# Message parts stored as consecutive bf16 elements, with the middle part rounded on ScalarE, in a graph network layer

## The reference, cut to what matters

```
msg  = concat([x[dst], edge_attr])            # 206250 x 128
h    = relu(msg @ W1a.T + b1a) @ W1b.T + b1b  # 206250 x 64
sums = segment_sum(h, src, 6250)              # and counts, for the mean
agg  = sums / max(counts, 1)
z    = relu(concat([x, agg]) @ W2a.T + b2a) @ W2b.T + b2b
out  = layernorm(x + concat([z, x]) @ Wr.T + br)
```

## Time and profile before

| | |
|---|---|
| median of 3 runs | 1581.24 us |
| the profiled execution | 1581.64 us, span 1580.0 us |
| PE matmul busy | 1534.2 us, 97% |
| PEld weight load busy | 1261.8 us, 80% |
| DVE busy | 1395.8 us, 88% |
| ACT busy | 942.6 us, 60% |
| POOL busy | 1061.9 us, 67% |
| mean granted TensorE clock | 0.992 |

### The profile page before, as it was taken

How to read it: one execution, slowest core, us unless ns; L and a number is a source line. 1 busy time by engine, 2 the same in 40 slices (tenths; PEclk the granted TensorE clock), 3 DMA queues, 4 the chain that set the end, 5 groups by cost and what they waited for, 6 DMA issues and landing times.

```text
span 1580.0 us, 41462 instructions
## 1 busy us (share of the span) xinstructions
PE 1534.2 (97%) x13337; PEld 1261.8 (80%) x13337; DVE 1395.8 (88%) x3954; ACT 942.6 (60%) x1808; POOL 1061.9 (67%) x929
## 2 busy tenths in 40 slices
PE   9899999999999999999999999999999999995897
PEld 6678878888887887877878788888888888884786
DVE  5799999999989999999988989999999999884886
ACT  2476767677677676767767775555555555563222
POOL 2366667666666676666767778777777777876542
PEclk9999999999999999999999999999999999997999
DMA  7566656666666666666656669889989989866997
GB/s 207 163 163 161 173 158 165 167 165 165 158 174 160 163 173 161 163 167 167 163 157 171 170 166 315 273 279 294 286 281 292 277 271 290 279 193 198 364 364 236
DMA packets 135497, 335.37 MB, mean 212 GB/s; under 512 B 36506, under 2 KB 69565, under 8 KB 129016
## 3 DMA queue, kind: packets, MB, share of 16 engines
q0 software_dynamic: 53184, 224.62, 45.3%
q1 hardware_dynamic: 81028, 104.02, 25.7%
q10 hardware_dynamic: 1076, 4.09, 1.0%
HBM read 213.07 MB, written 119.52 MB: 210 GB/s over the span
## 4 chain that ended last, share of the span: by engine, by line
PE 86%; DMA 4%; POOL 3%; DVE 2%; issue 2%; ACT 1%; SPq 0%; POOLq 0%; DVEq 0%; ACTq 0%
PE HH L543 22%; PE MS L552 18%; PE PA L568 14%; PE PBk L568 13%; PE RK L581 8%; DMA gbuf<-region,idx 3%; POOL region L1295 2%; PE RK L661 2%; PE RK L666 2%; PE CK L628 2%; PE PA L581 2%; DVE OH L1133 1%; DMA kb<-keyd 0%; POOL gbuf L1323 0%; PE PA L700 0%
## 5 line engine op out<-in xcount | busy, mean ns | idle before, releaser
L1295 POOL DMA_INDIRECT region<-stg,dest x806 | 930.5, 1154 | 417.2 <-ACT stg L852 246.8
L552 PE MATMUL MS<-W,hT 128*128 128x64 f32 x3224 | 508.1, 258 | 4.5 <-DVE pos L1017 3.0
L552 PEld LDWEIGHTS MS<-W,hT 128*128 128x128 f32 x3224 | 466.6, 191 | 6.5 <-DVE pos L1017 3.3
L543 PE MATMUL HH<-eab,pw 128*128 128x512 f32 x806 | 433.2, 619 | 1.7 <-ACT hT L806 1.7
L1012 DVE TENSOR_SCALAR M<-pos_of,pos 128x384 bf16<-128x384 int16 x1612 | 409.1, 316 | 0.2
L852 ACT ACTIVATE stg<-PA 120x585 bf16<-120x585 f32 x403 | 266.6, 661 | 184.7 <-PE PA L568 184.3
L568 PE MATMUL PA<-Z,M 128*128 128x195 bf16 x2418 | 354.3, 254 | 3.8 <-DVE M L1012 1.5
L568 PE MATMUL PBk<-Z,M 128*128 128x195 bf16 x2418 | 354.0, 254 | 0.2 <-ACT stg L852 0.2
L568 PEld LDWEIGHTS PA<-Z,M 128*128 128x128 bf16 x2418 | 230.1, 106 | 122.1 <-issue 117.2
L806 ACT ACTIVATE hT<-HH 128x512 f32<-128x512 f32 x403 | 240.8, 598 | 127.4 <-PE HH L543 127.0
L852 ACT ACTIVATE stg<-PBk 120x585 bf16<-120x585 f32 x403 | 266.1, 660 | 51.1 <-PE PBk L568 49.2
(11 more groups left out here) (207 smaller groups left out, 1386.1 us busy)
## 6 DMA issues: line engine op xcount, KB each, us to landing
eab<-in_ea SPq DMA_DIRECT2D x201, 256.0 KB
kb<-keyd SPq DMA_DIRECT2D x201, 128.0 KB
pw<-ptab SPq DMA_DIRECT2D x403, 32.0 KB
region<-stg,dest POOLq DMA_INDIRECT x806
gbuf<-in_xt ACTq DMA_DIRECT2D x6, 422.5 KB
ptab<-OH SPq DMA_DIRECT2D x7, 256.0 KB, 2.4
gbuf<-region,idx POOLq DMA_INDIRECT x98, 8.4
eab<-in_xt SPq DMA_DIRECT2D x12, 130.0 KB
```

The lines of the kernel that those rows point to most:

```text
L543: e.matmul(HH[:, :], pw[:, q % 4, :], eab[:, c % NB, at_q:at_q + GE], start=True, stop=True).then_inc(s_h, 1)
L552: ins = e.matmul(MS[:, o:o + D], hT[:, q % 2, 128 * j:128 * j + 128], W[:, W_1B:W_1B + D], start=True, stop=True)
L1295: e.indirect_dma_start(region[s], bass.IndirectOffsetOnAxis(ap=dest[:, g:g + 1], axis=0), stw[:, g % NS, :], None).then_inc(s_sc[g % NS], 16)
```

## The change

Z becomes a bf16 tile in which the three parts of a message column (65 elements each) are consecutive, [128, 2, 8, 3, 65], so the 195 moving columns of `permute` are contiguous. A float32 tile Zr of one pair holds the remainder.

- `copy_x` and `copy_id` write bf16, so ScalarE rounds the high part.
- `rest` writes MS minus the high part into Zr. It waits in addition for the middle part of the pair before (s_mid), since Zr has one buffer.
- `middle_part` is new on ScalarE: it copies Zr to part 1 as bf16. It stands in the turn after relu(2m), ahead of evict(2m-3).
- `low` waits for s_mid instead of s_r, and writes Zr minus the middle part as bf16. It stands behind the four places of quad 2m-2 and ahead of onehot(m+1).
- The memset of the ones follows the new layout, and there is one more semaphore.

```diff
-        Z = sb("Z", [128, 2, 3, 8, PART])
-        Zb = Z[:, :, :, :, :].bitcast(bf16)
+        Z = sb("Z", [128, 2, 8, 3, PART], bf16)
+        Zr = sb("Zr", [128, 8, D])
...
-                                                Zb[:, q // 2 % 2, :, 4 * (q % 2) + 2 * h + t, 1::2],
+                                                Z[:, q // 2 % 2, 4 * (q % 2) + 2 * h + t, :, :],
...
                     def copy_x(m):
                         n = 4 * of_pair(m)
                         e.wait_ge(s_msg, m + 1)
-                        e.activation(Z[:, m % 2, 0, 0:n, 0:D],
+                        e.activation(Z[:, m % 2, 0:n, 0, 0:D],
                                      MS[:, 0:n * D].rearrange("p (j f) -> p j f", f=D), ACT.Copy).then_inc(s_x, 1)
+
+                    def middle_part(m):
+                        n = 4 * of_pair(m)
+                        e.wait_ge(s_r, m + 1)
+                        e.activation(Z[:, m % 2, 0:n, 1, 0:D], Zr[:, 0:n, :], ACT.Copy).then_inc(s_mid, 1)
...
                             relu(2 * f)
+                        if m - 1 in front:
+                            middle_part(front[m - 1])
...
                         e.wait_ge(s_x, m + 1)
-                        e.tensor_tensor(Z[:, m % 2, 1, 0:n, 0:D],
-                                        MS[:, 0:n * D].rearrange("p (j f) -> p j f", f=D),
-                                        Zb[:, m % 2, 0, 0:n, 1:2 * D:2], ALU.subtract).then_inc(s_r, 1)
+                        if m >= 1:
+                            e.wait_ge(s_mid, m)
+                        e.tensor_tensor(Zr[:, 0:n, :], MS[:, 0:n * D].rearrange("p (j f) -> p j f", f=D),
+                                        Z[:, m % 2, 0:n, 0, 0:D], ALU.subtract).then_inc(s_r, 1)
 
                     def low(m):
                         n = 4 * of_pair(m)
-                        e.wait_ge(s_r, m + 1)
-                        e.tensor_tensor(Zb[:, m % 2, 2, 0:n, 1:2 * D:2], Z[:, m % 2, 1, 0:n, 0:D],
-                                        Zb[:, m % 2, 1, 0:n, 1:2 * D:2], ALU.subtract).then_inc(s_l, 1)
+                        e.wait_ge(s_mid, m + 1)
+                        e.tensor_tensor(Z[:, m % 2, 0:n, 2, 0:D], Zr[:, 0:n, :],
+                                        Z[:, m % 2, 0:n, 1, 0:D], ALU.subtract).then_inc(s_l, 1)
...
                         if m - 1 in front:
                             rest(front[m - 1])
-                            low(front[m - 1])
                         if 0 <= 2 * m - 2 < NQ:
                             places(2 * m - 2, 0)
                             places(2 * m - 2, 1)
+                        if m - 1 in front:
+                            low(front[m - 1])
                         if m + 1 in front:
                             onehot(front[m + 1])
```

More of the change, by code:

```diff
@@ L310, in _ @@
                 e.memset(ind[:, 62:63], 1.0)
-                e.memset(Z[:, :, 1, :, 64:65], 1.0).then_inc(p_t, 1)
+                e.memset(Z[:, :, :, 1, 64:65], 1.0).then_inc(p_t, 1)
             @block.vector
@@ L393, in program @@
          s_oh, s_h, s_relu, s_msg, s_x, s_r, s_l, s_M, s_pA, s_pB, s_eA, s_eB,
-         s_OHv, s_acc, s_ad, s_nt, s_tx, s_zt, s_z1, s_r1, s_y, s_sq, s_var, s_rt, s_fin, s_sw, s_zr, s_zs, s_id, s_P, s_pz, s_pt, s_xr, s_rest) = [
-            sem(f"s{i}") for i in range(47)]
+         s_OHv, s_acc, s_ad, s_nt, s_tx, s_zt, s_z1, s_r1, s_y, s_sq, s_var, s_rt, s_fin, s_sw, s_zr, s_zs, s_id, s_P, s_pz, s_pt, s_xr, s_rest, s_mid) = [
+            sem(f"s{i}") for i in range(48)]
         again = [*s_ch, *s_pw, *s_sc, *s_ga, *s_gb, *s_tab, *s_kw, *s_nx, *s_ob, *s_xo,
@@ L399, in program @@
                  s_oh, s_h, s_relu, s_msg, s_x, s_r, s_l, s_M, s_pA, s_pB, s_eA, s_eB,
-                 s_OHv, s_acc, s_ad, s_nt, s_tx, s_zt, s_z1, s_r1, s_y, s_sq, s_var, s_rt, s_fin, s_sw, s_zr, s_zs, s_id, s_P, s_pz, s_pt, s_xr, s_rest]
+                 s_OHv, s_acc, s_ad, s_nt, s_tx, s_zt, s_z1, s_r1, s_y, s_sq, s_var, s_rt, s_fin, s_sw, s_zr, s_zs, s_id, s_P, s_pz, s_pt, s_xr, s_rest, s_mid]
         TURNS = range(FIRST, NP + 2)
@@ L813, in copy_id @@
                         k = 8 * m % (16 * BQ)
-                        e.activation(Z[:, m % 2, 0, 0:n, D], lid[:, k:k + n], ACT.Copy)
+                        e.activation(Z[:, m % 2, 0:n, 0, D], lid[:, k:k + n], ACT.Copy)
                     def copy_x(m):
```

## The result

The changed kernel takes 1577.47 us (median of 8 runs, 1576.36 to 1579.41), the kernel before, run beside it, 1582.31 us (median of 8). The ratio is 0.9972, 95% interval [0.9961, 0.9983]: faster by 4.4 us, or 0.3%. I had said 12.7 us, and 1569 us. The profiled execution took 1577.92 us, its span is 1576.3 us and its granted clock 0.990 (before 0.992).

What follows compares the result with a forecast made beforehand. TensorE was taken as the bound. Gains of 8.7 us in plain and 6.7 in class-sum turns, less 2.7 in chain turns, make 12.7 us off 1581.64, so 1569 us; the 8-in-10 range was 1554 to 1590.

Steps and rivals of the forecast that it cites:

- P = R+2.38: In a plain turn, permute's start (P) was forecast 2.38 us after the start of rest (R); before the change 2.37.
- The middle part takes 0.63 us and is hidden: ScalarE's new copy of 512 elements from SBUF, 0.60 to 0.66 us, was to end while VectorE does the places.
- Low takes 0.72 and starts at R+1.57: VectorE's low, 750 ns before, was to take 0.72 us, starting 1.57 us after rest starts, behind four places.
- first rival: Low fully hidden: permute's releasers finish before TensorE wants them; gain about 26 us, 1556 us; chance 0.22.
- 5.7 ns for each of 4836 matmuls, 27.6 us: Contiguous columns were to cut each permute matmul on TensorE from 92 to 86.3 ns, 24 matmuls a turn.
- The upper end, 9 ns each: Upper bound of the layout's gain on TensorE, 43 us, if all 195 columns went at 0.43 ns each.
- A plain turn of 6.05, a gain of 0.06 in 145 turns: 8.7 us: Turns without class sum or late chain were to go from 6.11 to 6.05 us, TensorE waiting 0.08 for low.
- 8 chain turns lose 0.33 each, 2.7 us: Turns where a block's chain makes rest late and already held TensorE: permute starts later, each losing 0.33 us.
- a slack of 0.39 us: How much later than needed permute's releasers could come in a plain turn before the change without TensorE waiting.
- 49 class-sum turns gain the whole 0.137, 6.7 us: Turns with 2.6 us of class-sum matmuls ahead of permute: low not late, so TensorE's full layout gain remains.
- the layout buys nothing: Rival: contiguous columns gain TensorE nothing, plain turns 0.01 us longer; 5 us slower, 1586 us; chance 0.15.
- low becomes the bound: Rival: slower middle part and low make permute late, turn 0.10 us longer; 12 us slower, 1593 us; chance 0.20.

Runs made afterwards that it cites:

- e4: Changed kernel with the middle part copied for only 8 of 64 columns, the others left out: 1579.56 us, ratio 0.9986.
- e2: Changed kernel with the new layout alone: order of before, no middle part, low subtracts the high part: 1565.03 us, ratio 0.9887 to the kernel before.
- e1: Changed kernel with low between the two pairs of places instead of behind all four: 1575.19 us, ratio 0.9947 to the kernel before.
- e16: Changed kernel with middle part and low split per quad up to turn 144, first half of low behind two places: 1571.22 us, ratio 0.9931.
- e10: Changed kernel with 8 instead of 120 rows in 99 of 806 scatters: ratio 1.0829 where the kernel before takes 1753 to 1780 us.
- e12: The changed kernel itself, no edit, on a chip where the kernel before takes 1753.34 us: 1887.02 us, ratio 1.0724.

## Why the prediction was right or wrong, point by point

The mechanism held: a layout that speeds TensorE up, and an order that makes it wait for low. Three terms of the sum were mis-sized. The forecast's 153 turns without class sums were to gain 6.0 us, which is 4.7 for turns 20 to 140, and 0.2 were measured there; for 46 class-sum turns to 6.3, and 3.2 were measured. The plain turn gains half of what was put down, because part of the pitch is lost among the messages. The late turns are twice as many as before, where the sum had them as 8. And the class-sum turns don't get the whole pitch.

- **TensorE is the bound and P = R+2.38.** Right: the median of P - R is 2.371 over turns 8 to 141.
- **The middle part takes 0.63 us and is hidden.** Right: 631 ns, and e4 gains nothing by cutting it to 263.
- **Low takes 0.72 and starts at R+1.57.** Errors that cancel, so that P = R+2.38 is luck: it takes 682 ns, starts at R+1.63 in the median (bounds 1.51 to 1.60), and the matmul follows its end by 0.06 and not by 0.09. The start was counted from places of 0.99 us, which is right in the 15 plain turns without a stretched place (R+1.52); in 89 the GpSimd instruction stretches one. Before, most of that stretching seems to have fallen on onehot, which nobody waits for: 115 of its 202 instructions last over 780 ns, each with the end of a GpSimd instruction 489 to 493 ns ahead of its own, and 7 after the change (mean 855 ns, now 756). The prediction moved instructions along VectorE's queue without asking what GpSimd does at their new time. The 15 turns with unstretched places are its first rival come true, low hidden and the turn 6.00 us.
- **5.7 ns for each of 4836 matmuls, 27.6 us.** The pitch is right where permute's matmuls stand together (92 against 86 ns), but half of them stand among the messages, whose gaps take part of the gain back: 0.115 instead of 0.137 us for a turn. 202 x 0.022 = 4.4 us. Of the remaining 23.2 us e2 gets 17.9; its 17 late turns (5.7 us against 3.3) are 2.4 more, and 3 us are not accounted for. The upper end, 9 ns each, is also a slip: 195 columns at 0.43 ns are 84 ns, 8 below 92.
- **A plain turn of 6.05, a gain of 0.06 in 145 turns: 8.7 us.** The median turn is 6.08, before 6.12: a gain of 0.03. The wait of TensorE, forecast at 0.08, is 0.066 in the median; of the half of the gain ahead of P nothing is left, as forecast, and of the half behind P 0.03 instead of 0.068, the same messages again.
- **8 chain turns lose 0.33 each, 2.7 us.** The mechanism is right, and the count was not. The 8 added up six waits in the weight loads' row and two in the matmuls'; by the start of permute 11 turns were late before. P goes from R+1.98 to R+2.26 in them and not to R+2.38, since their places aren't stretched by much, and their waits grow from 3.3 to 6.5 us, 0.29 each. And 11 more turns have become late, with 4.0 us: a slack of 0.39 us was used up, so those are late too in which `rest` came up to 0.39 us late without harm. I counted the first kind alone, and 7.2 us of waiting came of both. So the mean turn, over turns 8 to 141 without 124, gains 0.007 us (6.269 to 6.262), and the waiting at P is 0.098 longer (0.130 against 0.032).
- **49 class-sum turns gain the whole 0.137, 6.7 us.** Turns 148 to 194 gain 3.2 us, 0.070 each. That low isn't late there is right: the waits at permute add up to 0.4 us in these 46 turns, before, after and in e2. The layout alone gains 4.7. The 1.5 us between them are nearly one event: in front of one class sum, at 1130 us, TensorE is idle for 1.34 us in the change, 1.64 in e1 and 1.49 in e16, and never over 0.2 before or in e2. What ended it the trace doesn't tell. That e2 gets 0.10 a turn and not 0.137 is the messages' 0.022 again, and the rest is open.

The sum by what was measured in the two profiled executions, 1580.0 and 1576.3 us: up to turn 1 -0.6, turns 1 to 20 -2.2, turns 20 to 140 -0.2, to turn 148 +0.6, class-sum turns to 194 -3.2, and from there to the end +1.9, together -3.7. The +1.9 behind turn 194 was put at nothing in the prediction (e2 and e16 have -0.8 and -0.6 there, e1 +1.8); what causes it was not looked for. Of the rivals, "low fully hidden" fails by P in 89 of 106 plain turns; "the layout buys nothing" fails by e2; "low becomes the bound" fails by P = R+2.37, but what it priced, a release that has no slack left, is what took the gain in the late turns. The line rule of the Trainium skill ("Advanced Engine Details and Errata", section Memory Cachelines), by which a 4-byte stride costs nothing, does not agree with ScalarE's writes of the same 512 values, 754 ns at every second bf16 element against 607 in a row. Nor does it agree with e2, if the stride and not the three pieces is what TensorE pays for.

## What to carry to other kernels

When a move uses up a slack, price it over the distribution of how late its input comes, not over the turns that wait already: the waiting grew by 0.098 us in the mean turn, and 11 late turns became 22. When an instruction gets faster inside a mixed stream, measure its pitch next to its neighbours; over a third of the gain of a twelve-matmul block (42 ns are left of 68) went to the messages between them. When instructions move in VectorE's queue, look at where GpSimd's end will fall: 0.12 us of stretching decided between a plain turn of 6.00 and one of 6.08. A release that needs two engines in a row was cheapest cut in halves that overlap (e16, 0.9931 against 0.9972), until the eviction that stands behind the copy on the second engine became what is waited for; where the kernel before takes 1753 to 1780 us, the halves were the dearest (1.10 against 1.07).

## What the runs showed of the hardware that was not expected

- A VectorE instruction of 128x384 that starts 0.3 to 0.5 us ahead of the end of a GpSimd indirect DMA instruction lasts up to 0.54 us instead of 0.31; all 159 that last over 0.38 in the traces of before and after end 57 to 90 ns behind that end. Those that start 0.5 us or more ahead of it, beside the same instruction, last 0.30 to 0.32.
- The indirect DMA instruction takes GpSimd 887 ns for 8 rows and 995 for 120 (means of the same 99 instructions in e10 and e12).
- ScalarE's copy of 512 from PSUM takes 598 ns to float32, 607 to bf16 in a row and 754 to bf16 at every second element.
- The same kernel pair has a ratio of 0.9972 on one chip and 1.0724 on another, with VectorE's and ScalarE's instructions as short and VectorE starting on TensorE's results over a microsecond later. A result of 0.3% holds for the chips on which it was taken.
